# A fused retention and mixture-of-experts layer: the first pipeline step is reordered, and two small products move from VectorE to GpSimd

## The reference

```python
# 1. retention: 8 heads of 16, chunks of 64 rows
x = x + retention(layernorm(x) @ Wq, layernorm(x) @ Wk, layernorm(x) @ Wv) @ Wo
#    inside a chunk: (q k^T * decay) v; between chunks: a state S, decayed and updated per chunk
# 2. mixture of 8 experts, hidden size 256
xt = layernorm(x)
probs = softmax(xt @ Wg)                        # 8 experts
top_w, top_i = top_k(probs, 2)
top_w = top_w / (sum(top_w) + 1e-8)
combine = one_hot(top_i) weighted by top_w      # rows x 8, two entries not zero
h = square(relu(xt @ W1[e])); y = h @ W2[e]     # for all 8 experts
x = x + sum over e of combine[:, e] * y[e]
```

## Time and profile before

| | |
|---|---|
| median of 3 runs | 288.34 us (287.51 to 290.0) |
| the profiled execution's own time | 286.49 us |
| its span in the trace | 284.6 us |
| TensorE busy | 268.1 us (94%) |
| VectorE, ScalarE, GpSimd busy | 212.5, 184.9, 208.2 us |

### The profile page before, as it was taken

How to read it: one execution, slowest core, us unless ns; L and a number is a source line. 1 busy time by engine, 2 the same in 40 slices (tenths; PEclk the granted TensorE clock), 3 DMA queues, 4 the chain that set the end, 5 groups by cost and what they waited for, 6 DMA issues and landing times.

```text
span 284.6 us, 8898 instructions
## 1 busy us (share of the span) xinstructions
PE 268.1 (94%) x3614; PEld 210.4 (74%) x3614; DVE 212.5 (75%) x505; ACT 184.9 (65%) x306; POOL 208.2 (73%) x205
## 2 busy tenths in 40 slices
PE   7999886869999999999999999999999999999993
PEld 5675665658886788778886788778886788788882
DVE  2879258695859956795959956795959769997781
ACT  2566557545794677665794677665794577587770
POOL 2246949787887978968887978969887858585542
PEclk9999999979999999999999999999999999999999
DMA  7438064021240240403440240102520251143102
GB/s 231 149 99 260 14 215 149 2 70 54 107 136 13 81 173 13 150 7 119 141 142 10 78 172 17 76 11 90 167 74 2 79 176 21 65 152 123 61 0 76
DMA packets 13576, 26.86 MB, mean 94 GB/s; under 512 B 1120, under 2 KB 6496, under 8 KB 13536
## 3 DMA queue, kind: packets, MB, share of 16 engines
q1 hardware_dynamic: 13536, 26.30, 27.4%
HBM read 24.07 MB, written 2.23 MB: 92 GB/s over the span
## 4 chain that ended last, share of the span: by engine, by line
PE 53%; POOL 15%; DVE 12%; issue 9%; ACT 6%; DMA 3%; POOLq 1%; DVEq 0%; ACTq 0%; SPq 0%
POOL act_lo L1125 11%; PE h_ps L346 7%; PE h_ps L348 6%; PE h_ps L347 6%; PE y_ps L367 5%; PE y_ps L361 5%; PE y_ps L362 5%; PE bank L500 4%; DVE attn L677 3%; DVE spread L756 3%; DVE root L752 3%; PE bank L512 3%; POOL r_denom L1086 2%; ACT act_f L981 2%; PE bank L522 2%
## 5 line engine op out<-in xcount | busy, mean ns | idle before, releaser
L1125 POOL TENSOR_TENSOR act_lo<-act_f,act_hi 128x512 fp32r<-128x512 f32 x112 | 145.7, 1325 | 49.6 <-ACT act_f L981 40.9
L773 DVE SCALAR_TENSOR_TENSOR act_s<-h_ps,scale 128x1024 f32<-128x1024 f32 x64 | 77.7, 1216 | 28.4 <-issue 15.5
L976 ACT ACTIVATE act_hi<-act_s 128x1024 fp32r<-128x1024 f32 x64 | 68.5, 1070 | 32.1 <-DVE act_s L773 31.8
L981 ACT ACTIVATE act_f<-act_s 128x1024 f32<-128x1024 f32 x64 | 67.8, 1060 | 0.0
L346 PE MATMUL h_ps<-x_hi,w_lo 128*128 128x512 f32 x128 | 54.4, 425 | 1.9 <-DVE attn L677 1.0
L361 PE MATMUL y_ps<-act_hi,w_lo 128*128 128x512 f32 x128 | 52.4, 409 | 0.0
L348 PE MATMUL h_ps<-x_hi,w_hi 128*128 128x512 f32 x128 | 51.2, 400 | 0.0
L347 PE MATMUL h_ps<-x_lo,w_hi 128*128 128x512 f32 x128 | 50.9, 398 | 0.0
L362 PE MATMUL y_ps<-act_hi,w_hi 128*128 128x512 f32 x128 | 50.5, 395 | 0.0
L367 PE MATMUL y_ps<-act_lo,w_hi 128*128 128x512 f32 x128 | 40.3, 396 | 0.1
L346 PEld LDWEIGHTS h_ps<-x_hi,w_lo 128*128 128x128 f32 x128 | 24.3, 190 | 10.4 <-issue 3.4
(11 more groups left out here) (123 smaller groups left out, 398.2 us busy)
## 6 DMA issues: line engine op xcount, KB each, us to landing
scale<-scratch SPq DMA_DIRECT2D x32, 512.0 KB, 4.1
x_t_in<-x_tr SPq DMA_DIRECT2D x8, 256.0 KB, 4.7
x_all<-x SPq DMA_DIRECT2D x8, 256.0 KB, 4.6
out<-out_sb SPq DMA_DIRECT2D x8, 256.0 KB, 4.0
scale<-w SPq DMA_DIRECT2D x1, 768.0 KB, 5.0
cst<-constants SPq DMA_DIRECT2D x1, 417.0 KB, 4.8
cst<-constants SPq DMA_DIRECT2D x1, 296.0 KB, 5.4
cst<-constants SPq DMA_DIRECT2D x1, 260.0 KB, 2.8
```

What stands on the lines that cost most here:

```text
L773: nc.vector.scalar_tensor_tensor(out=act_s[:, u % 2], in0=h_ps[:, u % 2], scalar=0.0, in1=scale[:, f % 2, e].unsqueeze(1).to_broadcast([P, ...
L976: nc.scalar.activation(act_hi[:, u % 4], act_s[:, u % 2], ACT.Square).then_inc(act_hi_ready, 1)
L981: nc.scalar.activation(act_f[:, u % 2], act_s[:, u % 2], ACT.Square).then_inc(act_f_ready, 1)
L1125: nc.gpsimd.tensor_tensor(act_lo[:, u % 4, n], act_f[:, u % 2, n], act_hi[:, u % 4, n].bitcast(F32), ALU.subtract).then_inc(pool_low_ready, 1)
```

## The change

The change touches step 0 (f = 0), the prologue just before it, and, in all steps, two operations of the routing chain.

- SyncE: the first quarter of tile 0's scales is loaded as soon as its store has landed; before, it also waited until tile 1's attention outputs were done (`av_done` 2).
- TensorE, prologue: `transpose_roots(0)` and `w1_product(0, 1)` come after the first outputs of tile 1 and `project_k(2)`; `w1_product(0, 4)` comes ahead of `project_v(2)`.
- TensorE, step 0: `transpose_roots(1)` moves from slot 11 to slot 14.
- VectorE, step 0: `scale_h(0, 2)` comes ahead of `decay_q(2)`; `mark_chosen(1)` moves behind `scale_h(0, 3)`; the last sum (`combine`) moves behind `scale_h(0, 6)`.
- All steps: `root` and `spread` are made by GpSimd, right behind `r_denom`; VectorE keeps the sum and waits for `spread`. `mark_chosen` waits until GpSimd has used the last `chosen`; GpSimd waits, before `spread`, until VectorE has used the last one.
- ScalarE, step 0: `square` of unit 0 comes ahead of `mask_q(2)`; `exponentiate(1)` ahead of `square` of unit 2.
- GpSimd, step 0: the routing chain's first part comes ahead of `low(1)`; `root_denominators`, the two products and `low_x(1)` come behind `low(3)`.

```diff
--- before.py
+++ after.py
@@ -264,9 +264,7 @@
                 sp.wait_ge(root_stored, DMA * (s + 1))
 
             def load_scale(s, j):
-                if j == 0 and s == 0:
-                    sp.wait_ge(av_done, 2)
-                elif j == 0 and s == 1:
+                if j == 0 and s == 1:
                     sp.wait_ge(piece_low, PIECES)
                     sp.wait_ge(w2_low, 4)
                 elif j == 0 and s >= 2:
@@ -562,7 +560,7 @@
                     if n == 15:
                         outputs_within(a, (2, 3))
                         outputs_before(a)
-                if p < TILES and n == 11:
+                if p < TILES and n == (14 if f == 0 else 11):
                     transpose_roots(p)
 
             pe.wait_ge(zeroed, 1)
@@ -590,10 +588,10 @@
             state_updates(1)
             center_piece(4)
             w1_product(0, 0)
-            w1_product(0, 1)
-            transpose_roots(0)
             outputs_within(1, (0, 1))
             project_k(2)
+            transpose_roots(0)
+            w1_product(0, 1)
             outputs_within(1, (2, 3))
             outputs_before(1)
             transpose_k(2)
@@ -605,8 +603,8 @@
             project_q(2)
             w1_product(0, 2)
             w1_product(0, 3)
+            w1_product(0, 4)
             project_v(2)
-            w1_product(0, 4)
             w2_product(0)
             for f in range(TILES):
                 for e in range(EXPERTS):
@@ -733,6 +731,7 @@
                 ranked(2)
                 nc.vector.tensor_copy(best_f[:], best_at[:, :, 0:TOP]).then_inc(rank_step, 1)
                 ranked(3)
+                dve.wait_ge(spread_step, SPREAD_STEPS * s)
                 iota = cst[:, C_IOTA:C_IOTA + EXPERTS].unsqueeze(1).to_broadcast([P, GROUPS * TOP, EXPERTS])
                 nc.vector.tensor_tensor(
                     chosen[:].rearrange("p g k e -> p (g k) e"), iota,
@@ -746,18 +745,8 @@
                 nc.vector.tensor_reduce(total[:], expd[:], AX_X, ALU.add)
                 nc.vector.tensor_reduce(pair_sum[:], expd[:, :, 0:TOP], AX_X, ALU.add).then_inc(total_ready, 1)
 
-            def spread_roots(s):
-                dve.wait_ge(r_denom_ready, s + 1)
-                dve.wait_ge(expd_ready, s + 1)
-                nc.vector.tensor_tensor(root[:], half_expd[:], r_denom[:].unsqueeze(2).to_broadcast([P, GROUPS, TOP]),
-                                        ALU.mult).then_inc(spread_step, 1)
-                dve.wait_ge(spread_step, SPREAD_STEPS * s + 1)
-                dve.wait_ge(rank_step, RANK_STEPS * (s + 1))
-                nc.vector.tensor_tensor(
-                    spread[:].rearrange("p g k e -> p (g k) e"), chosen[:].rearrange("p g k e -> p (g k) e"),
-                    root[:].rearrange("p g k -> p (g k)").unsqueeze(2).to_broadcast([P, GROUPS * TOP, EXPERTS]),
-                    ALU.mult).then_inc(spread_step, 1)
-                dve.wait_ge(spread_step, SPREAD_STEPS * s + 2)
+            def combine(s):
+                dve.wait_ge(spread_step, SPREAD_STEPS * (s + 1))
                 if s >= 1:
                     dve.wait_ge(root_t_done, s)
                 nc.vector.tensor_reduce(combine_r[:], spread[:].rearrange("p g k e -> p e g k"), AX_X, ALU.add
@@ -817,7 +806,7 @@
             add_chosen(0)
             mark_chosen(0)
             mask_updates(1)
-            spread_roots(0)
+            combine(0)
             scan_states(1)
             decay_k(2)
             add_attention(1)
@@ -827,11 +816,10 @@
                 low(u - 1)
                 if f == 0:
                     scale_h(f, 1)
+                    scale_h(f, 2)
                     decay_q(a)
-                    scale_h(f, 2)
                     statistics(p, 1)
                     rank_experts(p)
-                    mark_chosen(p)
                 else:
                     if p < TILES:
                         add_attention(p)
@@ -851,8 +839,10 @@
                         add_chosen(p)
                 scale_h(f, 3)
                 low(u + 2)
-                if 1 <= f and p < TILES:
-                    spread_roots(p)
+                if f == 0:
+                    mark_chosen(p)
+                elif p < TILES:
+                    combine(p)
                 if a < TILES:
                     decay_scores(a, decay_order(a)[0:1])
                 scale_h(f, 4)
@@ -1013,12 +1004,12 @@
                 a, p, u = f + 2, f + 1, EXPERTS * f
                 if f == 0:
                     high_x(p)
+                    square(u)
                     mask_q(a)
-                    square(u)
                     square(u + 1)
                     copy_v(a)
+                    exponentiate(p)
                     square(u + 2)
-                    exponentiate(p)
                 else:
                     square(u)
                     if a < TILES:
@@ -1085,6 +1076,20 @@
                     pool.wait_ge(spread_step, SPREAD_STEPS * (s - 1) + 1)
                 nc.gpsimd.tensor_tensor(r_denom[:], denom[:, 2], minus_half[:], ALU.pow).then_inc(r_denom_ready, 1)
 
+            def spread_roots(s):
+                pool.wait_ge(r_denom_ready, s + 1)
+                pool.wait_ge(expd_ready, s + 1)
+                nc.gpsimd.tensor_tensor(root[:], half_expd[:], r_denom[:].unsqueeze(2).to_broadcast([P, GROUPS, TOP]),
+                                        ALU.mult).then_inc(spread_step, 1)
+                pool.wait_ge(spread_step, SPREAD_STEPS * s + 1)
+                pool.wait_ge(rank_step, RANK_STEPS * (s + 1))
+                if s >= 1:
+                    pool.wait_ge(combine_ready, s)
+                nc.gpsimd.tensor_tensor(
+                    spread[:].rearrange("p g k e -> p (g k) e"), chosen[:].rearrange("p g k e -> p (g k) e"),
+                    root[:].rearrange("p g k -> p (g k)").unsqueeze(2).to_broadcast([P, GROUPS * TOP, EXPERTS]),
+                    ALU.mult).then_inc(spread_step, 1)
+
             def low_x(s):
                 r = s % X2T_RING
                 pool.wait_ge(x_hi_ready, s + 1)
@@ -1137,6 +1142,7 @@
             shift_logits(0)
             low_x(0)
             root_denominators(0)
+            spread_roots(0)
             pool.wait_ge(combine_ready, 1)
             low_piece(2)
             low_piece(3)
@@ -1147,12 +1153,10 @@
                 a, p, u = f + 2, f + 1, EXPERTS * f
                 if f == 0:
                     low(u)
-                    low(u + 1)
                     root_variance(p, 1)
                     shift_logits(p)
-                    low_x(p)
+                    low(u + 1)
                     low(u + 2)
-                    root_denominators(p)
                 else:
                     low(u - 1)
                     low(u)
@@ -1163,8 +1167,13 @@
                     low(u + 1)
                     if p < TILES:
                         root_denominators(p)
+                        spread_roots(p)
                     low(u + 2)
                 low(u + 3)
+                if f == 0:
+                    root_denominators(p)
+                    spread_roots(p)
+                    low_x(p)
                 low(u + 4)
                 low(u + 5)
                 if a + 1 < TILES:
```

## The result

The changed kernel takes **278.91 us** (278.16 to 280.48, 4 runs) against 288.22 (287.51 to 290.0, 4 runs): a ratio of 0.9675, 95% interval 0.9614 to 0.9736. Its profiled execution took 278.63 us, with a span of 276.6, against 286.49 and 284.6.

What follows compares the result with a forecast made beforehand. TensorE was taken to bound the kernel, with most to win in step 0's waits and clock drop. Terms −2.4 + 0.2 − 3.6 − 1.4 + 0.75 − 1.0 = −7.4 us: 281.0 from 288.34, range 279.2 to 284.8.

Steps and rivals of the forecast that it cites:

- (h): Later steps: with the pair on GpSimd, TensorE's 0.2 us wait for scaled scores goes in five steps, −1.0 us.
- the step from the profiled execution to the median: Whole kernel: the saving worked out on the profiled 286.49 us was applied to the median, 288.34 us, giving 281.0.
- (a to c): Step 0 up to the scores: earlier first quarter, unit 2's scaling and scores start at 46.9 instead of 49.32, −2.4 us.
- (a): Ahead of step 0's first scaling: the first quarter lands 1.7 us ahead of need, TensorE's 0.77 wait goes, −0.8 us.
- (d): Step 0, first scaled scores: `mark_chosen` now stands ahead of them, so they come slightly late, +0.2 us.
- (e): Step 0, transposition of tile 1's roots: nothing waits behind the state updates any more, −3.6 us.
- (g): Step 0, GpSimd: unit 4's low part is done at 60.3, TensorE wants it at 59.6, +0.75 us.
- (f): Step 0 behind the roots' wait: without the idling the clock holds, about 6.5 products at 0.21 us extra, −1.4 us.
- the first (a part of the wait comes back): Step 0's chain through ScalarE and GpSimd runs late ahead of `w2_product(4)`: saving 4.2, about 284 us; chance 0.18.
- The second: Step 0: roots reach TensorE 3 us behind slot 14, the clock falls again, about 286 us; chance 0.08.
- The third: All steps: the pair is dear on GpSimd, so the kernel is slower, 298 us at 4.9 us per pair; chance 0.04.
- The fourth: Step 0: the quarter lands no earlier or v still waits, (a to c) fall away: −5.0, 283.3; within first rival's range.

Runs made afterwards that it cites:

- the gap filled by zeros: The kernel before with 16 products of zeros on TensorE ahead of step 0's transposition of the roots: 286.37 us, ratio 0.9947.
- the longer pauses: The changed kernel with 13, 14, 16, 18 and 20 unread small sums on VectorE ahead of the first scaled scores in five later steps: 283.22 us.
- the pair alone moved: The kernel before with only root and spread moved to GpSimd in all steps, step 0's order untouched: 282.6 us, ratio 0.9817.
- the better version: The changed kernel with GpSimd's x_lo behind unit 4's low part, roots' copy behind unit 5's squares, first square between x copies: 277.62 and 278.39 us without longest runs.

## Why the prediction fell short

The mechanism held in the main: every wait that was to go went, the new one came where it was expected, the pair took 0.20 and 0.30 us, and the clock stayed up. Two steps failed. **The term of the sum that was mis-sized is (h)**, the later steps: I took the idle time shown, 0.2 in each of five, for the price of the stop. It was 0.46, and −2.27 us in place of −1.0. **The other is the step from the profiled execution to the median**, "with the same saving it becomes 281.0": it let stand the 1.85 us by which the median of before lay above its profile. In the changed kernel that distance is 0.3 (278.91 and 278.63). This step is some 1.6 of the 2.1 us between forecast and result; profile against profile the kernel gained 7.9 (286.49 to 278.63) where 7.4 was forecast.

The other terms:

- *(a to c)* −2.12 for −2.4. The sum is nearly right, its parts are not: (a), costed at −0.8 by itself, is worth nothing, since putting its wait back only moved idling from the next wait to this one. Nor did the quarter have the 1.7 us in hand that its reasoning gave it, but −0.3 to +0.3; that no wait was left there was in part luck.
- *(d)* nothing for +0.2: the scaled scores came in time.
- *(e)* −3.78 for −3.6; the 0.1 of the transposition itself, which is in (g) now, is among it. So this long stop, behind the short products of the state updates, cost hardly more than the 3.61 shown.
- *(f)* −1.23 for −1.4 between the two profiles. The prediction halved the 0.42 us between two products at the low clock to 0.21 at the full one; the rows show 0.23 there, so each product had lost 0.19 and not 0.21. Against the median the term was too small: 20 of the 35 runs of before reported a lower clock than the profiled one, and their median is 1.6 us above that of the others. I read the term from one execution and carried it over to the median. That this is the whole of the 1.6 above is not shown, since runs of one clock differ by as much; that the gap filled by zeros lowered the median by 1.5 speaks for it.
- *(g)* +1.32 for +0.75: GpSimd came 0.96 late by the trace, and the stop cost the quarter more (the product of the low part comes 1.36 behind the one ahead of it in place of 0.23); the moved transposition is the rest.

Together the stages moved −8.08 us where −7.45 was forecast. (h) at its measured size would have made the forecast 279.7, and the range, moved with it, would have held the result; so would the range moved by the 1.6 of the other step. That the range was too narrow below was an error of its own: its lower end took away new waits and allowed for a shift between runs, but no removed wait was allowed to be worth more than it showed.

Of the rivals, the first (a part of the wait comes back) happened in its place and at 1.3 us, of which the forecast held 0.75. The second came only when the slot was put back. The third fell with the first GpSimd row: for these two small operations the trace shows 0.50 us on GpSimd against 2.5 on VectorE. The Trainium skill (GPSIMD Engine Reference, section 4.1) has two-input work on a tile take about twice as long on GpSimd; these rows show the contrary. That VectorE's 2.5 were mostly waiting for GpSimd is inferred, from its own sum over 64 elements at 0.27, and was not tested. The fourth didn't happen.

## What to carry to other kernels

Price a stop of a busy TensorE from the starts of the products on either side and not from the idle time shown: between these 128×512 products it was about a quarter of a microsecond more at every stop measured, which makes a row of small waits worth twice what the list of waits says. Compare kernels stage by stage from the same points of the program; here stages repeat within 0.02 us while the whole wanders by two. Read the granted clock of every run, too, and not of the profiled one alone, before a saving seen there is carried over to the median. And before a wait is costed at its length, look for the next one on the same chain: of two waits in a row with slack between them, removing the first may be worth nothing.

## What was not expected of the hardware

- A stop that the list of waits does not show at all cost 0.30 us (step 2 of the longer pauses).
- The same store of 16 KB took 1.4 us to landing before, 2.7 and 2.6 in the two profiles of the changed kernel, and 2.8 and 1.4 in those of the better version; why was not found.
- Behind the same wait of 2.2 us ahead of the scores, the granted clock fell to 0.50 with the gap filled and with the pair alone moved, and did not in the profile of before.
- TensorE stopped at one place of step 1 for nothing that the profile shows, for 1.32 us with the pair alone moved and for 0.2 in the better version (both times), and not at all in the changed kernel. What the versions differ in there was not found.
